# Ten groups of float32 turns on TensorE: products with the identity in 32-column tiles in place of whole transposes

## The chip, the cores and the metric

The kernel runs on one core of one Trainium2 chip. The metric is the device time of one execution in microseconds (us), smaller is better. The profile is one execution recorded by the hardware profiler; its span runs from the first to the last instruction, and the execution's own time is a little longer than the span.

## What is computed

Four sequences of 512 tokens with 128 features go through one post-norm layer: attention with 16 heads of 8 features, a relative-position term that is added to the softmax's result, two layer norms, and then a mixture of 32 small experts of which each token takes its best 4.

```python
attn = softmax(einsum('bhqd,bhkd->bhqk', x @ Wq, x @ Wk) * e ** -0.5)
out = einsum('bhqk,bhkd->bhqd', attn + bias, x @ Wv)     # bias from rel_table
x1 = layernorm(x + layernorm(out, eps=1e-3) * gamma + beta)
sim = (x1 @ hasher_w.T) @ keys.T                          # 32 values a token
w = softmax(top_k(sim, 4))
proj = silu(x1 @ values_down[k]);  o += (proj @ values_up[k]) * w[k]
y = layernorm(x1 + x1 + o * scale)
```

## The kernel before

Four batches are worked through in rounds t = 0 to 3, each of 16 steps u (4 groups of 4 heads, times 4 blocks of 128 keys), and a tail follows. In one step TensorE makes

- four groups of scores `st_ps` (function `scores`, one head each, keys on the partitions). ScalarE takes the exponential of each into `probs` (L801), out of three PSUM banks in turn;
- four groups of scores `sm_ps` (`maximum_scores`) for heads some steps ahead, with the queries on the partitions. VectorE reduces each to its row maximum, `neg_max` (L947), and the two banks of `sm_ps` are used in turn, so each such group waits until the maximum before the last one is taken. The maxima reach the queries' stack later as extra rows, through GpSimd, a small turn ("shift") and a DMA;
- two halves of the product with the values, `ov_ps` (`values`, `value_half`, L1311).

All these products are written by `tiled` (L1253, the matmul itself on L1256): the 128 columns of the weights are cut into four matmuls of 32 columns, each with its own 32 partitions of the result. `whole` (L1266) makes one matmul of 128 columns; `turn` (L1317) is a whole transpose, and `tiled_turn` (L1260) four transposes of 32 columns, which is used for bfloat16 only.

Between these groups stand the "jobs" of round t: `up0` to `up7` are the second layer of the experts for batch t-2, `down0` to `down7` the first layer for batch t-1, `w0` to `w7` spread the experts' weights over rows, `wt` and `shift0` to `shift3` are bfloat16 turns. Three kinds of job are float32 turns of a 128 x 512 tile in four blocks of 128 columns:

- `o0` (eight heads of batch t, one in each of rounds 0 to 3, into `si_ps`) and `o1` (the other eight heads of batch t-1, in rounds 1 to 3, into `mi_ps`). ScalarE copies `ov_ps` to `o_sb` (L812), TensorE turns it (L1378), and VectorE divides by the row sums (`attend`, L953: `rsum`, then `attn`);
- `x1t` (rounds 1 to 3, into `mi_ps`): GpSimd ends the second norm with L523, TensorE turns `x1` (L1390), ScalarE copies it to `x1_t` (L819), and TensorE makes `sim` from it (L1397).

The order on every engine is written out by hand: `JOBS`, `SECOND_JOBS` and `LAST_JOBS` (L165 to L178) say after which step a job stands, `PLACES` and its like where VectorE's steps stand. Round 0 is of kind FIRST, round 1 SECOND, round 2 EVERY and round 3 LAST_ONE. Each engine takes its instructions in order and waits on semaphores. The tail after round 3 has one more `o1` turn (L1577) and one `x1t`.

In the rows a name `out<-a,b` of a matmul lists the moving tile first and then the weights: `si_ps<-ident,o_sb` has `o_sb` as weights and the identity as moving tile. `128*32 128x512` says weights of 128 partitions by 32 columns and 512 moving columns. `x_t` stands for `x1_t` too, and `x` for `x1`.

Of the kernel before, what the change touches and what calls it, by code (L numbers as in the profile page):

```python
# [5 lines left out]
def bass_postln_attention_product_key_ffn(nc, x, w_q, w_k, w_v, rel_table, gamma, beta,  # L6
# [6 lines left out]
    B, S, E = x.shape  # L13
    H = rel_table.shape[1]
    D = E // H
    P = 128
# [33 lines left out]
    with ctx:  # L50
        def sb(name, shape, dt=F32):
            return ctx.enter_context(nc.sbuf_tensor(name, shape, dt))
# [8 lines left out]
        ident, ident_bf = sb("ident", [P, P]), sb("ident_bf", [P, P], BF16)  # L61
# [23 lines left out]
        o_sb = sb("o_sb", [P, S])  # L85
# [10 lines left out]
        x1, x1_t = sb("x1", [P, 2, C, E]), sb("x1_t", [P, S])  # L96
# [99 lines left out]
        def is_misc(n):  # L196

            return n[:2] != "up" and n not in SIDE

        def is_kept(n):  # L200

            return is_misc(n) and n[:4] != "down"

        def is_side(n):

            return n in SIDE
# [20 lines left out]
        def jobs_of(kind):  # L227
            return [n for u in range(U) for half in jobs_at(kind, u) for n in half if here(n, *kind)]

        def job(t, name, counted):  # L230

            before = 0 if counted is is_side else 1
            before += sum(counted(n) for kind in KINDS[:t] for n in jobs_of(kind))
            if t == B + 1:
                return before + 1
            names = jobs_of(KINDS[t])
            return before + sum(counted(n) for n in names[:names.index(name) + 1])
# [17 lines left out]
        def hidden_count(f, j):  # L255
            return f * FJ + (TAIL_DOWN.index(j) if f == B - 1 else j) + 1
# [54 lines left out]
        def pool_at(f, name):  # L311
            if name in LATE_POOL:
                if f < B - 2:
                    return f * len(LATE_POOL) + (LATE_POOL.index(name) + 1)
                return (B - 2) * len(LATE_POOL) + (LATE_POOL_TAIL.index(name) + 1)
            return f * len(POOL_STEPS) + ((POOL_TAIL if f == B - 1 else POOL_STEPS).index(name) + 1)
# [31 lines left out]
        def is0(t):  # L348
            return t == 0
# [873 lines left out]
        def _(pe):  # L1223
# [29 lines left out]
            def tiled(dst, weights, moving, **flags):  # L1253

                for n in range(weights.shape[-1] // TILE):
                    i = nc.tensor.matmul(dst[n * TILE:(n + 1) * TILE], weights[:, n * TILE:(n + 1) * TILE], moving,  # L1256
                                         **flags)
                return i

            def tiled_turn(dst, src, idn):  # L1260

                for n in range(src.shape[-1] // TILE):
                    i = nc.tensor.transpose(dst[n * TILE:(n + 1) * TILE], src[:, n * TILE:(n + 1) * TILE], idn)  # L1263
                return i
# [52 lines left out]
            def turn(dst, src, idn):  # L1317
                return nc.tensor.transpose(dst, src, idn)  # L1318

            def up(f, j, in_round):  # L1320


                if j == 0:

                    count = job(in_round, f"up{FJ - 1}", is_side) - 1
                    if count > 0:
                        pe.wait_ge(side_done, count)
                pe.wait_ge(weighed, hidden_count(f, j))
                for c in range(C):
                    i = tiled(si_ps[:, c * P:(c + 1) * P], hid[:, j, c * P:(c + 1) * P], up_sb[:, j, :],  # L1330
                              start=(j == 0 and c == 0), stop=(j == FJ - 1), skip_group_check=True)
                if j == FJ - 1:
                    i.then_inc(side_ready, 1)

            def tail_up_part(j, c):
                return nc.tensor.matmul(tail_y_bank(c, P), hid[:, j, c * P:(c + 1) * P], up_sb[:, j, :],  # L1336
                                        start=(j == TAIL_UP[0] and c % 2 == 0), stop=(j == TAIL_UP[-1]),
                                        skip_group_check=True)
# [14 lines left out]
            def misc(t, name, kind):  # L1353

                f = t - 1
                if name.startswith("up"):
                    up(t - 2, int(name[2:]), t)
                    return
                bank, ready = (si_ps, side_ready) if is_side(name) else (mi_ps, misc_ready)
                if is0(t) and name == "shift1":  # L1360
                    pe.wait_ge(last_copied, 2)

                if is_side(name):
                    count = job(t, name, is_side) - 1
                    if count > 0:
                        pe.wait_ge(side_done, count)
                else:
                    count = job(t, name, is_kept)
                    pe.wait_ge(misc_done, count - 1 if is_kept(name) else count)
                    names = [n for n in jobs_of(kind) if is_misc(n)]  # L1370
                    last = names[names.index(name) - 1] if names[0] != name else name
                    if last != name and last.startswith("down"):
                        pe.wait_ge(hidden_made, hidden_count(f, int(last[4:])))
                if name.startswith("o"):
                    n = int(name[1:])
                    pe.wait_ge(o_copied, (f if n == PAIRS - 1 else t) * PAIRS + n + 1)
                    for c in range(C):
                        i = turn(bank[:, c * P:(c + 1) * P], o_sb[:, c * P:(c + 1) * P], ident[:])  # L1378
                elif name.startswith("shift"):
                    g = int(name[5:])  # L1380
                    pe.wait_ge(shift_split, (t + 1 if g == 0 else t) * G + g + 1)
                    i = tiled_turn(mi_bf[:, 0:P], shift_parts[:].rearrange("p i n -> p (i n)"), ident_bf[:])
                elif name == "x1t":
                    if t < B:
                        pe.wait_ge(pool_step, pool_at(f, "bscale"))
                    for c in range(C):
                        if t == B:
                            pe.wait_ge(tail_normed, c + 1)
                            bank = mi_ps if c < C // 2 else ov_ps
                        i = turn(bank[:, c * P:(c + 1) * P], x1[:, f % 2, c, :], ident[:])  # L1390
                        if t == B and c == C // 2 - 1:
                            i.then_inc(half_turned, 1)
                elif name == "sim":

                    pe.wait_ge(misc_done, job(t, "x1t", is_kept))
                    for c in range(C):
                        i = tiled(bank[:, c * NE:(c + 1) * NE], x1_t[:, c * P:(c + 1) * P], sim_w[:],  # L1397
                                  start=True, stop=True)
                elif name == "wt":
                    pe.wait_ge(w_split, f + 1)  # L1400
                    pe.wait_ge(spread_made, PARTS)
                    for c in range(C):
                        i = tiled_turn(si_bf[0:PARTS * NE, c * P:(c + 1) * P],
                                       w_parts[:, c].rearrange("p i n -> p (i n)"), ident_bf[:])
                elif name in SPREAD:
                    pe.wait_ge(side_done, job(t, "wt", is_side))
                    i = spread_weights(bank[:, :], int(name[1:]))
                else:
                    j = int(name[4:])
                    if j == 0:  # L1410
                        pe.wait_ge(experts_loaded, 32)
                    i = tiled(mi_ps[:], down_sb[:, j * NJ:(j + 1) * NJ, :].rearrange("k n d -> k (n d)"), x1_t[:],
                              start=True, stop=True)
                i.then_inc(ready, 1)

            def spread_weights(bank, j, product=tiled):
                return product(bank, spread[:, j].rearrange("r n p -> r (n p)"), w_t[:], start=True, stop=True)
# [49 lines left out]
            for n in range(NWIN // P):  # L1467
                i = turn(mi_ps[:, n * P:(n + 1) * P], rel_win[:, n, :], ident[:])
# [13 lines left out]
            for kc in range(C):  # L1482
                i = nc.tensor.matmul(st_ps[:, 2, 0:CG * J * B * D], rel_t[:, LAST:LAST + P],
                                     v_all[:, kc, 0:CG * J].rearrange("p h b d -> p (h b d)"),
                                     start=(kc == 0), stop=(kc == C - 1))
# [85 lines left out]
            f = B - 1  # L1571
# [4 lines left out]
            for c in range(C):  # L1576
                i = turn(mi_ps[:, c * P:(c + 1) * P], o_sb[:, c * P:(c + 1) * P], ident[:])  # L1577
# [44 lines left out]
            for chunks in (FIRST_HALF, SECOND_HALF):  # L1622
                for j in TAIL_UP[-CHUNKED:]:
                    for c in chunks:
                        i = tail_up_part(j, c)
# [23 lines left out]
```

## Time and profile before

| | |
|---|---|
| time, median of 3 runs | 300.7 us (298.92 to 301.14) |
| time of the profiled execution | 301.16 us |
| its span | 299.1 us |
| TensorE busy | 278.4 us, 93% |
| VectorE busy | 235.5 us, 79% |
| ScalarE busy | 197.6 us, 66% |
| GpSimd busy | 130.9 us, 44% |

PE is TensorE's matmuls, PEld its weight loads, DVE is VectorE, ACT ScalarE, POOL GpSimd and SP the engine that issues DMAs. A matmul's duration in the trace reaches from its start to its result in PSUM; the next one starts long before, so what a group costs TensorE is read from its start to the start of the next group, not from its duration. The brackets at the end of a row of a timeline say how long the engine was idle before it and what ended that.

### The profile page before, as it was taken

To read this page: it belongs to the slowest core of one execution; us is meant where nothing else is said; L and a number is where in the kernel's file an instruction comes from. 1 tells how busy PE (TensorE), PEld (TensorE's weight loads), DVE (VectorE), ACT (ScalarE), POOL (GpSimd) and SP (SyncE) were. 2 spreads that over 40 slices of the span, in tenths; PEclk is the share of its full clock that TensorE was granted. 3 is DMA by queue.
4 is the path that set the end of the run, shared out by engine and by line. 5 is a ranking of instruction groups with operands and counts; after the bars stand their busy time and mean duration, and the time that the engine had idled before them with its cause. 6 is when DMAs were issued, how large, how long until landed. Compare 5 with 4: busy or idle time off the path is not lost.

```text
span 299.1 us, 10998 instructions
## 1 busy us (share of the span) xinstructions
PE 278.4 (93%) x4660; PEld 146.7 (49%) x4661; DVE 235.5 (79%) x517; ACT 197.6 (66%) x390; POOL 130.9 (44%) x218
## 2 busy tenths in 40 slices
PE   4969999999999989999999999999999999889992
PEld 2644433444434344444557554445565645367482
DVE  4767899989989978987787799987977864148854
ACT  3652487867776668689864876889656689941620
POOL 8476133110115641137556312189365031885852
PEclk9997999999999999999999999999999999999999
DMA  5565095264051202000403030006100000010011
GB/s 158 154 179 150 9 182 118 40 178 118 2 136 31 79 4 83 4 2 25 139 6 81 4 83 5 1 3 177 24 4 2 6 3 3 2 37 2 2 37 35
DMA packets 18574, 17.27 MB, mean 58 GB/s; under 512 B 6830, under 2 KB 16222, under 8 KB 18526
## 3 DMA queue, kind: packets, MB, share of 16 engines
q1 hardware_dynamic: 17856, 16.39, 21.6%
q8 instruction: 37, 0.61, 0.9%
q10 hardware_dynamic: 670, 0.19, 0.3%
q14 instruction: 11, 0.09, 0.1%
HBM read 12.18 MB, written 4.23 MB: 55 GB/s over the span
## 4 chain that ended last, share of the span: by engine, by line
PE 68%; DVE 12%; DMA 6%; ACT 5%; POOL 4%; issue 3%; SPq 1%; POOLq 0%; DVEq 0%
PE sm_ps L1256 16%; PE st_ps L1256 14%; PE ov_ps L1311 14%; PE mi_ps L1256 6%; PE si_ps L1256 5%; DVE neg_max L947 5%; DMA k_stack<-parts_dram 3%; ACT probs L801 2%; DMA wq_sb<-L_attn_Wq 2%; ACT w_rows L703 1%; PE si_ps L1336 1%; PE mi_ps L1318 1%; PE st_ps L1568 1%; PE sm_ps L1336 1%; PE st_ps L1442 1%
## 5 line engine op out<-in xcount | busy, mean ns | idle before, releaser
L947 DVE TENSOR_REDUCE neg_max<-sm_ps 128x1 f32<-128x512 f32 x256 | 166.4, 685 | 29.2 <-PE sm_ps L1256 24.9
L801 ACT ACTIVATE probs<-st_ps 128x512 f32<-128x512 f32 x256 | 138.2, 610 | 34.0 <-PE st_ps L1256 34.0
L1256 PE MATMUL sm_ps<-k_stack,q_stack 96*32 96x512 bf16 x984 | 97.1, 383 | 3.0 <-DVE neg_max L947 2.1
L1256 PE MATMUL st_ps<-q_stack,k_stack 128*32 128x512 bf16 x1024 | 88.6, 380 | 0.2 <-ACT probs L801 0.2
L1311 PE MATMUL ov_ps<-probs,v_cur 128*32 128x256 f32 x1024 | 76.4, 378 | 0.0
L1256 PEld LDWEIGHTS sm_ps<-k_stack,q_stack 96*32 96x32 bf16 x984 | 26.3, 94 | 50.6 <-DVE neg_max L947 33.9
L533 POOL TENSOR_TENSOR hid<-hid,w_rows 128x512 f32<-128x512 f32 x27 | 34.1, 1278 | 30.7 <-ACT w_rows L703 30.7
L1311 PEld LDWEIGHTS ov_ps<-probs,v_cur 128*32 128x32 f32 x1024 | 31.6, 110 | 22.7 <-ACT probs L801 0.4
L1256 PEld LDWEIGHTS st_ps<-q_stack,k_stack 128*32 128x32 bf16 x1024 | 27.7, 96 | 28.3 <-ACT probs L801 9.1
L1010 DVE SCALAR_TENSOR_TENSOR hid<-tanh_sb,mi_ps 128x512 f32<-128x512 f32 x24 | 16.3, 681 | 15.0 <-ACT tanh_sb L838 15.0
L1256 PE MATMUL mi_ps<-x_t,down_sb 128*32 128x512 f32 x192 | 25.1, 592 | 0.0
L1256 PE MATMUL si_ps<-up_sb,hid 128*32 128x128 f32 x768 | 24.1, 273 | 0.0
L1256 PEld LDWEIGHTS si_ps<-up_sb,hid 128*32 128x32 f32 x768 | 21.3, 110 | 2.7 <-issue 0.3
L838 ACT ACTIVATE tanh_sb<-mi_ps 128x512 f32<-128x512 f32 x24 | 14.6, 610 | 9.3 <-PE mi_ps L1256 9.3
L489 POOL CAST shift_parts<-neg_max 128x16 bf16<-128x16 f32 x16 | 3.1, 196 | 32.6 <-DVE neg_max L947 23.9
L703 ACT ACTIVATE w_rows<-si_ps 128x512 f32<-128x512 f32 x24 | 15.1, 628 | 0.8 <-PE si_ps L1256 0.6
L505 POOL COPY v_cur<-v_all 128x128 f32<-128x128 f32 x16 | 4.5, 290 | 22.0 <-PE ov_ps L1311 21.9
L1256 PE MATMUL si_ps<-w_t,spread 96*32 96x512 bf16 x96 | 9.6, 381 | 1.8 <-ACT w_rows L703 1.8
L703 ACT ACTIVATE x_t<-mi_ps 128x512 f32<-128x512 f32 (+1 forms) x4 | 2.2, 544 | 11.9 <-PE mi_ps L1318 11.9
L553 POOL TENSOR_TENSOR parts<-resid,parts 128x512 bf16<-128x512 f32 x6 | 6.8, 1156 | 6.9 <-ACT parts L703 6.9
L703 ACT ACTIVATE shift_rows<-mi_ps 48x128 bf16<-48x128 bf16 x16 | 4.3, 270 | 6.7 <-PE mi_ps L1263 5.9
L514 POOL TENSOR_SCALAR veps<-mv 128x4 f32<-128x4 f32 x6 | 1.4, 229 | 15.9 <-DVE mv L995 15.9
(189 smaller groups left out, 301.2 us busy)
## 6 DMA issues: line engine op xcount, KB each, us to landing
q_stack<-parts_dram SPq DMA_DIRECT2D x16, 288.0 KB
k_stack<-parts_dram SPq DMA_DIRECT2D x48, 96.0 KB
parts_dram<-parts SPq DMA_DIRECT2D x24, 128.0 KB, 2.4
x_sb<-L_attn_x SPq DMA_DIRECT2D x4, 256.0 KB, 4.6
out<-y_out SPq DMA_DIRECT2D x3, 256.0 KB, 2.3
down_sb<-L_ffn_values_down SPq DMA_DIRECT2D x1, 512.0 KB, 5.7
up_sb<-L_ffn_values_up SPq DMA_DIRECT2D x1, 512.0 KB, 7.9
rel_win<-rel_dram SPq DMA_DIRECT2D x1, 256.0 KB, 2.7
```

The source lines that it names most:

```text
L489: nc.gpsimd.tensor_copy(shift_parts[:, 0, :], m).then_inc(shift_chain, 1)
L505: nc.gpsimd.tensor_copy(v_cur[:, :, g * J:(g + 1) * J, first:first + D], v_all[:, :, g * J:(g + 1) * J, t, :]).then_inc(v_ready, 1)
L533: nc.gpsimd.tensor_tensor(hid[:, j], hid[:, j], w_rows[:, j], ALU.mult).then_inc(weighed, 1)
L553: nc.gpsimd.tensor_sub(parts[:, b, a, 2, :], resid[:, b % 2, a], parts[:, b, a, 1, :]) \
L703: return nc.scalar.activation(dst, src, ACT.Copy, scale=scale)
L801: nc.scalar.activation(probs[:, u % 2, j, :], st_ps[:, score_bank(u * J + j), :], ACT.Exp, scale=SCORE_SCALE).then_inc(probs_ready, 1)
L838: nc.scalar.activation(tanh_sb[:, j % 3, :], mi_ps[:], ACT.Tanh, scale=0.5).then_inc(act_step, 1)
L947: nc.vector.tensor_reduce(neg_max[:, g % 2, col:col + 1], sm_ps[:, c % 2, :], AX.X, ALU.max, negate=True).then_inc(max_ready, 1)
L1010: nc.vector.scalar_tensor_tensor(out=hid[:, j], in0=tanh_sb[:, j % 3, :], scalar=1.0, in1=mi_ps[:], op0=ALU.add, op1=ALU.mult).then_inc(hi ...
L1256: i = nc.tensor.matmul(dst[n * TILE:(n + 1) * TILE], weights[:, n * TILE:(n + 1) * TILE], moving, **flags)
L1311: i = nc.tensor.matmul(ov_ps[j * TILE:(j + 1) * TILE, part], v_cur[:, kc, g * J + j, :], probs[:, u % 2, j, part], start=(g % 2 == 0 and k ...
L1336: return nc.tensor.matmul(tail_y_bank(c, P), hid[:, j, c * P:(c + 1) * P], up_sb[:, j, :], start=(j == TAIL_UP[0] and c % 2 == 0), stop=(j ...
```

## The change

The four float32 transposes of each `o` job and of each `x1t` job in rounds 1 to 3 become matmuls with the same data as weights and the same identity as moving tile, cut by `tiled` into 32 weight columns each: 16 matmuls and 16 weight loads where there were 4 of each. `x1t` of the tail (t == B) keeps the whole transposes, and so do the tail's `o1`, the turns of the start and all bfloat16 turns.

```diff
                     pe.wait_ge(o_copied, (f if n == PAIRS - 1 else t) * PAIRS + n + 1)
                     for c in range(C):
-                        i = turn(bank[:, c * P:(c + 1) * P], o_sb[:, c * P:(c + 1) * P], ident[:])
+                        i = tiled(bank[:, c * P:(c + 1) * P], o_sb[:, c * P:(c + 1) * P], ident[:],
+                                  start=True, stop=True)
...
-                        i = turn(bank[:, c * P:(c + 1) * P], x1[:, f % 2, c, :], ident[:])
+                        if t < B:
+                            i = tiled(bank[:, c * P:(c + 1) * P], x1[:, f % 2, c, :], ident[:], start=True, stop=True)
+                        else:
+                            i = turn(bank[:, c * P:(c + 1) * P], x1[:, f % 2, c, :], ident[:])
```

Ten groups are rewritten: `o0` four times, `o1` three times, `x1t` three times. The other engines keep their instructions and their order.

TensorE around `o0` of round 1, before (a turn among the scores, a `down` job behind it):

```order
L1256 MATMUL sm_ps<-k_stack,q_stack 32x512 x4
L1311 MATMUL ov_ps<-probs,v_cur 32x256 x4
L1256 MATMUL sm_ps<-k_stack,q_stack 32x512 x4
L1318 MATMUL si_ps<-ident,o_sb 128x128 x4
L1256 MATMUL st_ps<-q_stack,k_stack 32x512 x4
L1256 MATMUL sm_ps<-k_stack,q_stack 32x512 x4
```

And in the changed kernel:

```order
L1256 MATMUL sm_ps<-k_stack,q_stack 32x512 x4
L1311 MATMUL ov_ps<-probs,v_cur 32x256 x4
L1256 MATMUL sm_ps<-k_stack,q_stack 32x512 x4
L1256 MATMUL si_ps<-ident,o_sb 32x128 x16
L1256 MATMUL st_ps<-q_stack,k_stack 32x512 x4
L1256 MATMUL sm_ps<-k_stack,q_stack 32x512 x4
```

Nothing changes its place: four matmuls of line 1318 have become sixteen of line 1256 at the same point, and no group around them has moved.

TensorE around `x1t` of round 1, before (the turn of the normed rows, then `sim`, which needs ScalarE's copy of it, and a shift):

```order
L1256 MATMUL sm_ps<-k_stack,q_stack 32x512 x4
L1318 MATMUL mi_ps<-ident,x 128x128 x4
L1256 MATMUL st_ps<-q_stack,k_stack 32x512 x4
L1256 MATMUL sm_ps<-k_stack,q_stack 32x512 x4
L1256 MATMUL mi_ps<-sim_w,x_t 32x32 x16
L1263 MATMUL mi_ps<-ident_bf,shift_parts 32x128 x4
```

And in the changed kernel:

```order
L1256 MATMUL sm_ps<-k_stack,q_stack 32x512 x4
L1256 MATMUL mi_ps<-ident,x 32x128 x16
L1256 MATMUL st_ps<-q_stack,k_stack 32x512 x4
L1256 MATMUL sm_ps<-k_stack,q_stack 32x512 x4
L1256 MATMUL mi_ps<-sim_w,x_t 32x32 x16
L1263 MATMUL mi_ps<-ident_bf,shift_parts 32x128 x4
```

Here too only the turn itself is another; two groups of scores still stand between it and `sim`.

## Rows read from the trace of the kernel before

**Rows 1.** The page: span, and busy time of three engines.

```profile
span 299.1 us, 10998 instructions
PE 278.4 (93%) x4660; PEld 146.7 (49%) x4661; DVE 235.5 (79%) x517; ACT 197.6 (66%) x390; POOL 130.9 (44%) x218
```

**Rows 2.** The page: the chain that ended last, share of the span by engine.

```profile
PE 68%; DVE 12%; DMA 6%; ACT 5%; POOL 4%; issue 3%; SPq 1%; POOLq 0%; DVEq 0%
```

**Rows 3.** Groups by line and shape, TensorE: shapes xcount | busy us, mean ns | idle.

```profile
L1256 PE MATMUL si_ps<-up_sb,hid 128*32 128x128 f32 x768 | 24.1, 273 | 0.0
L1318 PE MATMUL si_ps<-ident,o_sb 128*128 128x128 f32 x16 | 2.6, 286 | 0.0
...
L1256 PEld LDWEIGHTS si_ps<-up_sb,hid 128*32 128x32 f32 x768 | 21.3, 110 | 2.7 <-issue 0.3
```

**Rows 4.** Timeline of TensorE, round 1 around `o0`: start us, us, instruction.

```profile
122.41 0.39 PE L1256 MATMUL sm_ps<-k_stack,q_stack 96*32 96x512 bf16 x4
122.72 0.66 PE L1318 MATMUL si_ps<-ident,o_sb 128*128 128x128 f32 x4
123.31 0.40 PE L1256 MATMUL st_ps<-q_stack,k_stack 128*32 128x512 bf16 x4
...
124.62 0.39 PE L1256 MATMUL st_ps<-q_stack,k_stack 128*32 128x512 bf16 x4
124.95 0.40 PE L1256 MATMUL sm_ps<-k_stack,q_stack 96*32 96x512 bf16 x4
```

**Rows 5.** Timeline of TensorE, round 2, `up` jobs between scores and behind a shift.

```profile
150.43 0.40 PE L1256 MATMUL sm_ps<-k_stack,q_stack 96*32 96x512 bf16 x4
150.66 1.05 PE L1256 MATMUL si_ps<-up_sb,hid 128*32 128x128 f32 x32
151.53 0.39 PE L1256 MATMUL st_ps<-q_stack,k_stack 128*32 128x512 bf16 x4
...
153.71 0.23 PE L1263 MATMUL mi_ps<-ident_bf,shift_parts 128*32 128x128 bf16 x4
153.76 1.04 PE L1256 MATMUL si_ps<-up_sb,hid 128*32 128x128 f32 x32
```

**Rows 6.** Timeline of TensorE, round 2, `o0` behind a shift.

```profile
180.47 0.23 PE L1263 MATMUL mi_ps<-ident_bf,shift_parts 128*32 128x128 bf16 x4
180.64 0.65 PE L1318 MATMUL si_ps<-ident,o_sb 128*128 128x128 f32 x4
```

**Rows 7.** Timeline of TensorE, round 1 behind `o1`.

```profile
87.60 0.63 PE L1318 MATMUL mi_ps<-ident,o_sb 128*128 128x128 f32 x4
88.16 0.62 PE L1256 MATMUL st_ps<-q_stack,k_stack 128*32 128x512 bf16 x8
89.23 0.40 PE L1256 MATMUL sm_ps<-k_stack,q_stack 96*32 96x512 bf16 x4 [0.45 <-DMA k_stack<-parts_dram]
```

**Rows 8.** Timelines of TensorE and ScalarE around `x1t` of rounds 1 and 3.

```profile
107.11 0.63 PE L1318 MATMUL mi_ps<-ident,x 128*128 128x128 f32 x4 [0.49 <-POOL x L523]
107.78 0.60 ACT L703 ACTIVATE x_t<-mi_ps 128x512 f32<-128x512 f32 x1 [1.49 <-PE mi_ps L1318]
108.52 0.46 PE L1256 MATMUL mi_ps<-sim_w,x_t 128*32 128x32 f32 x32 [0.23 <-ACT x_t L703]
...
228.34 0.63 PE L1318 MATMUL mi_ps<-ident,x 128*128 128x128 f32 x4 [0.43 <-POOL x L523]
```

**Rows 9.** Timeline of VectorE at `o0` of round 1, `o1` of rounds 2 and 3.

```profile
122.61 0.68 DVE L947 TENSOR_REDUCE neg_max<-sm_ps 128x1 f32<-128x512 f32 x1
123.42 0.36 DVE L962 RECIPROCAL rsum<-si_ps 128x32 f32<-128x32 f32 x1
...
148.08 0.35 DVE L962 RECIPROCAL rsum<-mi_ps 128x32 f32<-128x32 f32 x1
...
148.86 2.76 DVE L947 TENSOR_REDUCE neg_max<-sm_ps 128x1 f32<-128x512 f32 x4
...
210.49 0.69 DVE L947 TENSOR_REDUCE neg_max<-sm_ps 128x1 f32<-128x512 f32 x1 [0.66 <-PE sm_ps L1256]
```

## The prediction

> **What bounds the kernel now.** I read the page first: TensorE is busy 93% of a span of 299.1 us [rows 1]. Then the chain of waits: 68% of it is TensorE, 12% VectorE, 6% DMA, 5% ScalarE [rows 2]. So time taken from TensorE inside the rounds is worth something, though not everywhere. The groups by shape give the ten turns as a small item: 16 turn matmuls into `si_ps` are 2.6 us of busy time [rows 3], four groups' worth, so some 6.5 us for all ten. What a group costs is read from the timeline, start to start, and that is where the rest of the working comes from.
>
> **The price of one turn now.** In round 1 the score group ahead of `o0` starts at 122.41, the turn at 122.72 and the next score group at 123.31 [rows 4]. A score group ahead of another tiled group takes 0.23 (150.43 to 150.66, [rows 5]), in most places 0.22. Here it takes 0.31: 0.09 is lost on going into the whole-array turn. The turn itself takes 0.59. Behind a shift it is alike: shift to `up` is 0.05 (153.71 to 153.76, [rows 5]), shift to turn 0.17 (180.47 to 180.64, [rows 6]), so 0.12 lost. Going in costs about 0.10. Where TensorE was idle before the turn, or held for a copy, nothing is lost on entry and the turn takes 0.56 (87.60 to 88.16, [rows 7]).
>
> **The price of one turn afterwards.** The trace has this very shape: the `up` jobs are float32 products, 128x32 weights, 128 moving columns, cut by the same function. 32 of them take 0.87 (150.66 to 151.53, [rows 5]), so 16 take 0.435, or 27 ns each, and they start behind a score group or a shift without the loss. One turn thus gives 0.59 + 0.10 - 0.435 = 0.25 us of TensorE where it is busy before, 0.56 - 0.435 = 0.125 where it is not. Its result is hardly sooner than that: last start at 15 x 27 ns = 0.41 plus 0.27 for one matmul [rows 3] is 0.68, against 0.63 to 0.66 from first start to end now [rows 4, 8]. I take them as equal, so a waiting reader gains only the earlier entry, 0.10.
>
> A rule speaks against this step. The Trainium skill, "Perfetto Trace Analysis", section on transposes, says that a logical transpose should be a transpose and not a standard matmul, since the transpose skips the arithmetic; "TensorE: Matmul & The Clock Gate", Terms, calls the transpose mode four times faster for float32. The rows of `up` disagree for tiled weights, where a block of 128x128 in four column tiles is a product in 4 x 27 = 109 ns, against 140 for a whole transpose (0.56 / 4, [rows 7]). By the rule the product would stream four times as long as the transpose and the change would lose; the third rival has the price.
>
> **What each of the ten gives to the end.** What follows the turn decides, and I went through the ten places in the timelines.
>
> 1. `o0`, round 0 (66.4 us): the pattern of [rows 6]. VectorE is short of maxima behind the turn, waits for the next score group, and is the bound afterwards. It starts 0.25 sooner. Kept: 0.25.
> 2. `o1`, round 1: two groups later TensorE waits for `k_stack`, until 89.23 [rows 7]. That transfer was asked for before the turn. Kept: 0.
> 3. `x1t`, round 1: TensorE waits for GpSimd's last norm step, then the path goes turn, ScalarE's copy, `sim`, for which TensorE is idle 0.23 [rows 8]. The faster turn only lengthens this idle time. Between -0.05 and 0.05; taken: 0.
> 4. `o0`, round 1: TensorE gains 0.25, but VectorE is already at the turn's door: its reciprocal starts at 123.42, as the turn ends [rows 9], behind a maximum that lasts until 122.61 + 0.68 = 123.29, and the score group at 124.95 already comes 0.33 behind the one ahead of it, so it waits for VectorE [rows 4]. VectorE can move by 0.13 at most. Kept: 0.13.
> 5. `o1`, round 2: VectorE comes from a maximum to the reciprocal at 148.08 without having waited for the turn, and its four maxima from 148.86 run on until 151.6 [rows 9]; the score groups in this stretch wait for them. An earlier turn moves none of it. Kept: 0.
> 6. `x1t`, round 2 (166.7 us): entered and left like [rows 4], GpSimd done before it, `sim` not waited for. Kept: 0.25.
> 7. `o0`, round 2 [rows 6]: VectorE lags but TensorE has no wait behind it. Kept: 0.25.
> 8. `o1`, round 3 (209.0 us): VectorE was idle 0.66 for the score group behind the turn, at 210.49 [rows 9], and it leads the chain from there. Kept: 0.25.
> 9. `x1t`, round 3: GpSimd decides the entry [rows 8], but three score groups and more stand between it and `sim`, which isn't waited for. Kept: 0.12.
> 10. `o0`, round 3 (243.1 us): no maxima any more; ScalarE is idle behind the turn for the score group and the `down` job and then bounds the rest of the round. Kept: 0.25.
>
> The sum is 0.25 + 0.13 + 0.25 + 0.25 + 0.25 + 0.12 + 0.25 = 1.50 us (places 1, 4, 6, 7, 8, 9, 10). Ten turns at full value would be 8 x 0.25 + 2 x 0.125 = 2.25 us. The profiled execution took 301.16 us (2.1 outside its span), which becomes 299.6; the median of the runs shown is 0.46 lower, 300.7, and becomes 299.2 us. The 240 added instructions (120 matmuls, 120 loads) I cost at nothing: the 32 small matmuls of `sim` all start and end within 0.46 us of waiting [rows 8], so nothing in handing them out is slower than the 27 ns.
>
> The gain on entry is weighed against a rule too. [Rows 4] show 0.09 into the turn and no loss out of it (0.59 against 0.56). The Trainium skill, "TensorEngine Tiling (Array Packing)", Key Properties, says that a change of tiling mode drains the engine. By full drains each busy entry would cost the score group's rest, 0.39 - 0.22 = 0.17, and so would each exit; with 0.17 at eight entries the ceiling would be 2.8 in place of 2.25, and the exit would need a next group at 123.38 and not at 123.31.
>
> **The rivals.**
>
> *Everything is kept (or more).* The waits that I hold against places 2 to 5 could move with TensorE, since the DMA's request, VectorE's steps and the next round all follow from earlier groups: then 2.2 us, 298.5. For it: the chain is two thirds TensorE [rows 2]. Against: rows 7 to 9 show other engines last at these places.
>
> *Little is kept.* Beyond the places above, every later wait for a maximum, for ScalarE's copies of the spread weights or for the stack can take back what an earlier turn gave. For it: VectorE is at 79% over all [rows 1] and gates score groups in every round. Then 0.5 us or less, 300.3.
>
> *The product streams like four transposes.* A score group of 512 columns takes 0.22, so 128 columns stream in 0.055, and `up` with 0.109 for a block goes over them twice. If this product went over them four times, a block would take 0.22 and a turn 0.88: 0.88 - 0.59 - 0.10 = 0.19 more at the eight and 0.32 at the two, 2.2 us in all, 302.9. It is slower, by less than 1%. Against it: `up` needs 0.435 with float32 on both sides. For it only that the identity is a moving tile here, which no tiled row shows.
>
> *The weight loads don't overlap, and it gets slower by over 1%.* The mechanism is in PEld: one load of 128x32 lasts 110 ns [rows 3]. If the loads of one turn stand behind each other, because each block comes back to the same four column tiles, a turn takes 16 x 110 = 1.76 us, 1.1 more than now, and ten cost 11 us, 312. It decides once the spacing of the sixteen is above (0.59 + 0.10) / 16 = 43 ns. Against it: `up` has the same return to the same tiles, at 27 ns, and 768 loads are busy 21.3 us [rows 3], 28 ns each.
>
> **How the numbers follow.** The forecast of 1 to 2 us has a chance of 0.50, everything kept 0.20, little kept 0.22, the slow stream 0.05, loads in a row 0.03. A change of under 1%, about 3 us, is about what a measurement of this kernel can't tell from none, and even the ceiling of 2.25 us is below that; only by a stray median of 0.5 us or more, or by a knock-on that I don't see, would it come out faster by over 1%: 0.11. Slower by over 1% is the last rival and a part of the one before: 0.05. Within 1%: 0.84. The likeliest case alone is 298.7 to 299.7. The range reaches from 297.7, the ceiling with 0.8 for the spread of medians (single runs spread over 2.2 us), to 301.3, which holds little kept and that spread.
>
> **What would show it.** In the changed profile a turn should be 16 matmuls of line 1256 with 0.43 to 0.44 to the next start, and the score group ahead of it 0.22, at eight places. The wait for `k_stack` in round 1 should grow from 0.45 to about 0.6, the idle time before `sim` in round 1 by about 0.12, and VectorE's stretch from 148.08 keep its distance to round 2's start. The span should be near 297.6. The forecast is wrong if a turn's spacing is over 43 ns a matmul, if ScalarE's copy of `x1_t` starts later than 0.67 behind the turn's start, or if the turns are as cheap as said and the span stays within 0.5 us of 299.1, or falls by more than 2.3.

## The result and the profile after

The changed kernel is slower: 304.0 us median of 15 runs against 301.3 for the kernel before, ratio 1.0092 (95% interval 1.0063 to 1.0121), some 2.8 us. Measured again beside its parts it was 303.1 against 300.7, 2.4 us between the medians and 1.8 by the ratio of 1.0061 (1.0024 to 1.0097). 299.2 had been forecast, a gain of 1.5.

The page of the changed kernel: span, and busy time of three engines, against [rows 1].

```profile
span 300.0 us, 11559 instructions
PE 279.6 (93%) x4941; PEld 152.6 (51%) x4941; DVE 235.2 (78%) x517; ACT 197.5 (66%) x390; POOL 131.0 (44%) x218
```

The prediction had 240 more instructions. There are 561, and 281 of them are matmuls: the 16 and 4 of the section on the change are counts of the program, not of the engine. The groups by shape of the changed kernel say where they are (busy us, mean ns | idle):

```profile
L1256 PE MATMUL si_ps<-ident,o_sb 128*32 128x128 f32 x128 | 4.2, 273 | 0.0
...
L1256 PE MATMUL mi_ps<-ident,x 128*32 128x128 f32 x96 | 3.2, 274 | 0.9 <-POOL x L523 0.9
L1256 PE MATMUL mi_ps<-ident,o_sb 128*32 128x128 f32 x96 | 3.2, 273 | 0.1
```

128 for four turns is 32 for a turn: 4 blocks x 4 column tiles x 2. A float32 product that stands once in the program is two matmuls on the engine, while a float32 transpose is one ([rows 3]: 16 for four turns of four blocks). 10 x (32 - 4) = 280 is what was added. [Rows 3] had said it of `up` too: 768 for the 24 `up` jobs are 32 for a job, and the 32 of [rows 5] are one job, not two. `sim` had shown it too, with x16 in the program's order and x32 in [rows 8].

The timeline of TensorE in the changed kernel, at `o0` of round 1, of [rows 4], and at `o0` of round 2, of [rows 6]:

```profile
121.61 0.39 PE L1256 MATMUL sm_ps<-k_stack,q_stack 96*32 96x512 bf16 x4
121.83 1.05 PE L1256 MATMUL si_ps<-ident,o_sb 128*32 128x128 f32 x32
122.70 0.39 PE L1256 MATMUL st_ps<-q_stack,k_stack 128*32 128x512 bf16 x4
...
124.00 0.39 PE L1256 MATMUL st_ps<-q_stack,k_stack 128*32 128x512 bf16 x4
124.48 0.40 PE L1256 MATMUL sm_ps<-k_stack,q_stack 96*32 96x512 bf16 x4
...
180.34 0.23 PE L1263 MATMUL mi_ps<-ident_bf,shift_parts 128*32 128x128 bf16 x4
180.40 1.04 PE L1256 MATMUL si_ps<-ident,o_sb 128*32 128x128 f32 x32
181.27 0.39 PE L1256 MATMUL st_ps<-q_stack,k_stack 128*32 128x512 bf16 x4
```

The turn takes 0.87 to the next start where 0.435 was forecast, and 0.59 was before. The entry came as forecast: 0.22 behind a score group in place of 0.31, 0.06 behind a shift in place of 0.17 (only at place 10, where it is 0.12, less was gained). The spacing is 27 ns, as forecast, but of 32 matmuls. Read from the start of the group ahead to the start of the group behind, TensorE pays 0.17 to 0.19 more at six turns (0.87 - 0.69 = 0.18), 0.30 to 0.32 at three (0.87 - 0.56 = 0.31; places 2, 3 and 9, where it was idle or held ahead of the turn) and 0.23 at place 10, 2.27 us in all.

The result of a turn comes later as well. It ends 1.05 to 1.08 behind the turn's first start, against 0.63 to 0.66 [rows 4, 8]. VectorE at `o0` of round 1 [rows 9], then ScalarE and TensorE at `x1t` of round 1 [rows 8], in the changed kernel:

```profile
121.81 0.69 DVE L947 TENSOR_REDUCE neg_max<-sm_ps 128x1 f32<-128x512 f32 x1
122.95 0.36 DVE L962 RECIPROCAL rsum<-si_ps 128x32 f32<-128x32 f32 x1 [0.45 <-PE si_ps L1256]
...
106.98 0.60 ACT L703 ACTIVATE x_t<-mi_ps 128x512 f32<-128x512 f32 x1 [1.96 <-PE mi_ps L1256]
...
105.84 1.08 PE L1256 MATMUL mi_ps<-ident,x 128*32 128x128 f32 x32 [0.49 <-POOL x L523]
...
107.72 0.46 PE L1256 MATMUL mi_ps<-sim_w,x_t 128*32 128x32 f32 x32 [0.36 <-ACT x_t L703]
```

VectorE, which came to the turn as it ended, now stands idle 0.45 before it, and the score group that waited 0.33 behind its predecessor comes 0.48 behind it (124.00 to 124.48). ScalarE's copy of `x1_t` starts 1.14 behind the turn's start, against 0.67, and TensorE's idle time before `sim` has grown from 0.23 to 0.36.

### How the stretches are compared

The profiled spans differ by only 0.9 us, less than the runs say. The missing part lies ahead of the first turn, in instructions that are the same in both. The stretches of granted clock of the kernel before and then of the changed one (columns: stretch; busy us of PE, PEld, DVE, ACT, POOL; PEclk; DMA share, GB/s):

```profile
22.00:30.00 8.00, 8.00 (x102) 4.08 (x101) 6.37 (x11) 2.10 (x3) 5.51 (x5) 0.79 0.60 151
```

```profile
22.00:30.00 8.00, 8.00 (x124) 4.24 (x128) 7.89 (x14) 2.23 (x4) 6.13 (x8) 1.00 0.67 162
```

The execution of before had TensorE at its lower level (1.2 GHz) for part of these 8 us, the changed one didn't, and it came to the shift ahead of the first turn at 65.08 in place of 66.19. The other traces go the same way: those with 1.00 in these 8 us reach that shift at 65.00 and 65.34, those with 0.68 to 0.81 between 65.95 and 68.35. From there to the tail's `o1` turn (265.39 and 266.20) both run at the full clock. That stretch is 199.20 us before, 201.12 in the changed kernel and 201.11 in a second profile of it: it repeats to 0.01, and it is 1.92 longer. I use it below, cut at the start of the group ahead of each turn. The places are numbered as in the prediction; each figure is the length of its piece less that of the kernel before, in us. The third and fourth columns of figures are experiments told below.

| place | forecast | changed kernel | half turns | read columns |
|---|---|---|---|---|
| 1 `o0` r0 | -0.25 | +0.17 | -0.26 | -0.20 |
| 2 `o1` r1 | 0 | -0.34 | +0.29 | +0.82 |
| 3 `x1t` r1 | 0 | +0.48 | +0.03 | -0.01 (whole) |
| 4 `o0` r1 | -0.13 | +0.33 | -0.08 | +0.01 |
| 5 `o1` r2 | 0 | +0.16 | -0.25 | -0.20 |
| 6 `x1t` r2 | -0.25 | +0.18 | -0.25 | +0.01 (whole) |
| 7 `o0` r2 | -0.25 | +0.19 | -0.25 | -0.17 |
| 8 `o1` r3 | -0.25 | +0.18 | -0.26 | -0.17 |
| 9 `x1t` r3 | -0.12 | +0.33 | -0.12 | -0.01 (whole) |
| 10 `o0` r3 | -0.25 | +0.24 | -0.14 | -0.11 |
| sum | -1.50 | +1.92 | -1.29 | -0.03 |

### The profile page after: what moved, and what is told of

It reads as the page before. It is cut to its first block, busy times and chain, and to the rows that moved or that the text cites. A ratio compares the mean times of both kernels' runs of the same rounds, so it can differ in the third digit from the quotient of the medians.

```text
span 300.0 us, 11559 instructions
## 1 busy us (share of the span) xinstructions
PE 279.6 (93%) x4941; PEld 152.6 (51%) x4941; DVE 235.2 (78%) x517; ACT 197.5 (66%) x390; POOL 131.0 (44%) x218
## 4 chain that ended last, share of the span: by engine, by line
PE 70%; DVE 12%; ACT 5%; DMA 4%; POOL 4%; issue 3%; SPq 1%; POOLq 0%; DVEq 0%
PE sm_ps L1256 16%; PE st_ps L1256 14%; PE ov_ps L1311 14%; PE mi_ps L1256 8%; PE si_ps L1256 7%; DVE neg_max L947 6%; ACT probs L801 2%; DMA wq_sb<-L_attn_Wq 1%; DMA k_stack<-parts_dram 1%; ACT w_rows L703 1%; PE si_ps L1336 1%; PE st_ps L1241 1%; PE st_ps L1572 1%; PE sm_ps L1336 1%; PE st_ps L1446 1%
## 5 line engine op out<-in xcount | busy, mean ns | idle before, releaser
L1311 PEld LDWEIGHTS ov_ps<-probs,v_cur 128*32 128x32 f32 x1024 | 32.3, 110 | 22.1 <-ACT probs L801 0.4
L1256 PEld LDWEIGHTS st_ps<-q_stack,k_stack 128*32 128x32 bf16 x1024 | 28.7, 96 | 26.2 <-ACT probs L801 8.2
L636 POOL TENSOR_TENSOR sdiff<-sim,top 128x128 f32<-128x128 f32 x3 | 1.2, 407 | 15.9 <-DVE top L1016 15.9
```

Of the source, the lines that this page charges most:

```text
L1311: i = nc.tensor.matmul(ov_ps[j * TILE:(j + 1) * TILE, part], v_cur[:, kc, g * J + j, :], probs[:, u % 2, j, part], start=(g % 2 == 0 and k ...
```

## The experiments

### The change once more, and its two parts

The changed kernel again, then only the outputs as tiled products (`x1t` whole), then only the normed rows (`o` whole). The second kernel's edit to the changed one:

```diff
-                        if t < B:
-                            i = tiled(bank[:, c * P:(c + 1) * P], x1[:, f % 2, c, :], ident[:], start=True, stop=True)
-                        else:
-                            i = turn(bank[:, c * P:(c + 1) * P], x1[:, f % 2, c, :], ident[:])
+                        i = turn(bank[:, c * P:(c + 1) * P], x1[:, f % 2, c, :], ident[:])
```

The third takes back the other half:

```diff
-                        i = tiled(bank[:, c * P:(c + 1) * P], o_sb[:, c * P:(c + 1) * P], ident[:],
-                                  start=True, stop=True)
+                        i = turn(bank[:, c * P:(c + 1) * P], o_sb[:, c * P:(c + 1) * P], ident[:])
```

> The changed kernel once more, beside its parts on one chip. Theory A (each float32 matmul of the source is two matmuls on the engine, so a turn is 32 matmuls and 0.87 us against 0.69 or 0.56): about 2.1 us above before, ratio 1.007, a turn of 0.87 in the trace. Theory B (the turns cost little at the end and most of the loss is half-clock stretches): the ratio varies with the granted clock, and the spans at equal clock are within 0.7 us of before.

> Only the seven output turns are tiled products, the three turns of normed rows are whole transposes. Theory A: 7 x 0.18 = 1.3 us above before, less about 0.2 at the one turn with a wait for a transfer behind it: 1.1 to 1.3, ratio 1.004. Theory B: within 0.5 us of before at equal clock.

> Only the three turns of normed rows are tiled products. Theory A: 0.87 - 0.56 = 0.31 at the two where TensorE was idle before, 0.18 at the third: 0.8 us above before, ratio 1.0027. Theory B: nothing measurable, since GpSimd decides the entry at two of the three.

Measured against before: the change 1.0061 (1.0024 to 1.0097), outputs only 1.0076 (1.0046 to 1.0106), rows only 1.0027 (0.9993 to 1.0060). In the stretch the outputs alone add 1.24 us and the rows alone 0.95, both without place 2; together they make 2.19, and the changed kernel has 2.26 without that place. So the parts add up. For the rows alone the interval holds 1, so that their loss is shown by the stretch and not by the runs. Theory B falls: half-clock stretches at the start move single spans by a us or two, but 1.92 and 1.91 stand in two traces at full clock.

Place 2 has to be read by itself. It holds the wait for `k_stack`, which differs from execution to execution: 0.45 in [rows 7], 0.86 and 1.33 in two of the experiments below, and none in the six other traces. The kernel with rows only is the same program as before up to this place, with a whole transpose here, and had no wait. TensorE at place 2, rows only and then the changed kernel:

```profile
90.31 0.62 PE L1256 MATMUL st_ps<-q_stack,k_stack 128*32 128x512 bf16 x8
90.76 0.39 PE L1256 MATMUL sm_ps<-k_stack,q_stack 96*32 96x512 bf16 x4
```

```profile
87.52 0.64 PE L1256 MATMUL st_ps<-q_stack,k_stack 128*32 128x512 bf16 x8
87.95 0.43 PE L1256 MATMUL sm_ps<-k_stack,q_stack 96*32 96x512 bf16 x4
```

Start to start that is 0.45 and 0.43, against 1.07 in [rows 7]. So the -0.34 in the table is a wait that happened to be absent and hides a loss. Without the wait the piece is 0.67 shorter than before with whole transposes (rows only), and 0.33 or 0.34 shorter with the tiled turn (both profiles of the change, and outputs only): there the turn costs 0.33, as the 0.31 has it. With that the change costs 2.26 + 0.33 = 2.59 us where the transfer isn't late, and the outputs alone 1.24 + 0.34 = 1.58, inside the interval of their ratio (1.4 to 3.2 us), where 1.24 lies below it.

### The product without the tiles

```diff
-                        i = tiled(bank[:, c * P:(c + 1) * P], o_sb[:, c * P:(c + 1) * P], ident[:],
+                        i = whole(bank[:, c * P:(c + 1) * P], o_sb[:, c * P:(c + 1) * P], ident[:],
                                   start=True, stop=True)
```

and the same for `x1t` in the rounds.

> All ten turns are products with the identity, but whole, 128 weight columns each, so the tiles are taken away and the product is left. Theory A (the product's two passes cost, not the tiles): 8 matmuls at 0.112 us as in the tail's whole products, 0.90 for a turn, and the loss of 0.10 on entry stays: 0.31 above before at eight, 0.34 at two, 3.2 us in all, ratio 1.010. Rival (the cutting into 32 columns costs): 0.56 to 0.6 for a turn and a time like before.

Measured 305.1 against 300.7, ratio 1.0153 (1.0107 to 1.0199). The timeline of TensorE in this kernel, `o0` of round 1:

```profile
124.79 0.39 PE L1256 MATMUL sm_ps<-k_stack,q_stack 96*32 96x512 bf16 x4
125.11 1.16 PE L1267 MATMUL si_ps<-ident,o_sb 128*128 128x128 f32 x8
126.20 0.40 PE L1256 MATMUL st_ps<-q_stack,k_stack 128*32 128x512 bf16 x4
```

Eight matmuls for four blocks: the doubling comes with the product, not with the tiles. They are 0.136 apart, though, not 0.112, so a turn takes 1.09 and not 0.90. The stretch is 4.39 longer than before where theory A had 3.2, and the runs say 4.6 (3.2 to 6.0). The groups by shape give the load of such a block, 191 ns, where a whole transpose has 140 and a tile 110:

```profile
L1267 PEld LDWEIGHTS si_ps<-ident,o_sb 128*128 128x128 f32 x32 | 3.9, 191 | 0.7 <-issue 0.6
```

The tail's whole products have loads as long (192) and a closer spacing (four in 0.45); why, I didn't test. The score group ahead takes 0.32 again, as ahead of a whole transpose. Of the three ways to turn a tile, then, each with its entry: whole transposes 0.69, tiled products 0.87, whole products 1.19. The cutting is the good part of the change and the product the bad one.

### The turn that the prediction had priced

Each of the ten turns makes only blocks 0 and 1 of four, so that it is 16 matmuls; the other half of the turned tile is left out.

```diff
-                    for c in range(C):
+                    for c in range(C // 2):
                         i = tiled(bank[:, c * P:(c + 1) * P], o_sb[:, c * P:(c + 1) * P], ident[:],
```

and the same for `x1t` in the rounds.

> Each of the ten tiled turns makes only two of its four blocks of 128 columns, so half of the turned tile is left out. 16 matmuls, 0.435: this is the turn as the prediction had counted it. If the accounting by places held and only the count was wrong, the stretch from the first turn to the tail's is 1.5 us shorter than before, ratio 0.995. Rival (costs are kept everywhere, gains are lost to the engine that comes next): less than 0.8 us shorter, ratio 0.9975 or more. Other rival: nearly all of 2.25 is kept, ratio 0.9925.

Measured 299.8 against 301.3, ratio 0.9942 (0.9905 to 0.9980). The stretch is 1.29 shorter, and 1.58 without place 2 (here with a wait of 0.86), where 1.50 had been forecast. The timeline of TensorE in this kernel, `o1` of round 2 (place 5), and VectorE at the same place:

```profile
147.70 0.39 PE L1256 MATMUL sm_ps<-k_stack,q_stack 96*32 96x512 bf16 x4
147.92 0.61 PE L1256 MATMUL mi_ps<-ident,o_sb 128*32 128x128 f32 x16
148.36 0.60 PE L1256 MATMUL st_ps<-q_stack,k_stack 128*32 128x512 bf16 x8
...
150.87 0.40 PE L1256 MATMUL sm_ps<-k_stack,q_stack 96*32 96x512 bf16 x4
```

```profile
148.15 0.69 DVE L947 TENSOR_REDUCE neg_max<-sm_ps 128x1 f32<-128x512 f32 x1 [0.62 <-PE sm_ps L1256]
148.75 0.35 DVE L962 RECIPROCAL rsum<-mi_ps 128x32 f32<-128x32 f32 x1
149.13 0.49 DVE L966 TENSOR_TENSOR attn<-mi_ps,rsum 128x128 f32<-128x128 f32 x2
149.54 2.51 DVE L947 TENSOR_REDUCE neg_max<-sm_ps 128x1 f32<-128x512 f32 x4
```

The turn is 0.44, as the sum had it. VectorE does stay in step with the maximum ahead of the turn, and yet the 0.25 isn't lost here: the piece up to the next turn is 0.25 shorter. The score group that VectorE holds up (150.87) had slack behind it, and the four maxima take 2.51 in place of 2.76: before, the second of them started 0.83 behind the first, behind the score group that it reads, and here 0.60.

### Twice the turn

```diff
-                    for c in range(C):
+                    for c in 2 * tuple(range(C)):
                         i = tiled(bank[:, c * P:(c + 1) * P], o_sb[:, c * P:(c + 1) * P], ident[:],
```

and the same for `x1t` in the rounds.

> Each of the ten tiled turns is made twice over, into the same bank; nothing is left out. One more turn is 32 matmuls, 0.87 us. If TensorE's time is the path at all ten places, the stretch from the first turn to the tail's grows by 8.7 us over the changed kernel, ratio to before 1.037. If other engines hide part of it, as at the wait for the stack in round 1, less: 7 us or under.

Measured 312.4 against 301.3, ratio 1.0372 (1.0336 to 1.0408). Over the changed kernel the stretch grows by 9.69 us. Nine of the ten pieces grow by 0.84 to 0.89, as long as one more turn of 0.87; none is hidden, not even at place 2, which had no wait in either trace. The tenth, place 8, grows by 1.87, because TensorE once stands idle without a releaser:

```profile
219.09 0.38 PE L1311 MATMUL ov_ps<-probs,v_cur 128*32 128x256 f32 x1 [0.89 <-issue]
```

No other trace of this case has that hole, and its cause stays open.

### Only the columns that are read

`attend` reads 9 of every 16 columns of a turned block: 8 features of a head and its row sum. The turn needs no others. On top of the kernel with the outputs only:

```diff
+            def read_columns(a):
+                return a.rearrange("p (n w) -> p n w", w=HALF_TILE)[:, :, 0:D + 1]
...
-                        i = tiled(bank[:, c * P:(c + 1) * P], o_sb[:, c * P:(c + 1) * P], ident[:],
-                                  start=True, stop=True)
+                        i = tiled(read_columns(bank[:, c * P:(c + 1) * P]), o_sb[:, c * P:(c + 1) * P],
+                                  read_columns(ident[:]), start=True, stop=True)
```

> A turn that could beat both: the output turns stay tiled products, but make only the 9 of every 16 columns that are read afterwards (8 features and the row sum of a head), 72 moving columns in place of 128; the turns of normed rows are whole transposes as before. Theory A1 (the 27 ns from matmul to matmul are two passes over the moving columns): 15 ns each, 0.49 for a turn of 32, so 0.59 + 0.10 - 0.49 = 0.20 less than before at six places, 1.2 us in all, ratio 0.996. Theory A2 (the 27 ns are the weight load, 110 ns shared by four tiles): the turn stays at 0.87 and the time is that of the kernel with tiled outputs only, 1.0076 of before.

Measured 300.1 against 301.3, ratio 0.9954 (0.9922 to 0.9985). The groups by shape and the timeline of TensorE in this kernel, the latter at `o0` of round 1 and behind `o1` of that round:

```profile
L1256 PE MATMUL si_ps<-ident,o_sb 128*32 128x72 f32 x128 | 2.8, 226 | 0.0
...
L1256 PEld LDWEIGHTS si_ps<-ident,o_sb 128*32 128x32 f32 x128 | 2.3, 109 | 0.2
```

```profile
122.39 0.69 PE L1256 MATMUL si_ps<-ident,o_sb 128*32 128x72 f32 x32
122.90 0.40 PE L1256 MATMUL st_ps<-q_stack,k_stack 128*32 128x512 bf16 x4
...
89.01 0.40 PE L1256 MATMUL sm_ps<-k_stack,q_stack 96*32 96x512 bf16 x4 [1.33 <-DMA k_stack<-parts_dram]
```

Still 32 matmuls and 32 loads of 109 ns, but 0.51 for the turn: 16 ns apart where it was 27. So the spacing follows the moving columns (theory A1), and the loads hide at this pace too. Without place 2 the stretch is 0.85 shorter than before, where 1.2 had been expected; place 4 keeps nothing, as VectorE starts on the turn's result only 0.04 sooner than before (0.97 behind the start of the score group ahead in place of 1.01). In this profile the wait for `k_stack` happened to be 1.33, so that the whole stretch is only 0.03 shorter, while the runs give 1.4 us.

## Why the prediction was wrong

- **The price afterwards: the step that failed.** "32 of them take 0.87, so 16 take 0.435" is true, but 16 was the count in the program, where the trace counts two matmuls for each. I compared the program's count of the turn with the trace's count of `up`. One `up` job has the same 16 products in the program as one turn, so its 0.87 was the price of a turn. With it the sum's own terms give 0.87 - 0.69 = +0.18 at eight and 0.87 - 0.56 = +0.31 at two. That is 2.06 us; the stretch measured 1.92, which was in part luck with the wait at place 2: 2.26 without that place, and 2.59 with it where no trace has the wait. Of the 2.59 TensorE pays 2.27 at the turns; 0.16 at place 3 and 0.14 at place 4 come on top. The count of eight and two was off as well: place 2 was held for a copy before the turn, so it belonged to those with 0.56.
- **The third rival, given 0.05, was the right one.** It had the product go over the columns four times, 0.055 us each, with 0.88 for a turn and 2.2 us for the ten. Measured are 0.87 and 1.9 to 2.6. What I held against it, `up` with 0.109 for a block, is 0.217 once the 32 are one job: four times 0.055, which fits two matmuls that go over them twice each. With 72 columns it is 0.51 / 4 = 0.13 for a block, and four times 0.22 x 72 / 512 is 0.12. A whole transpose takes 0.14 for a block, as long as its load of 140 ns; that the load is what holds it wasn't tested. The Trainium skill had the direction right in both places that the prediction set aside. "TensorE: Matmul & The Clock Gate", Terms, calls the transpose mode four times faster for float32; in time the runs show less, 0.14 against 0.217 for a block in tiles and 0.27 as a whole product. "Perfetto Trace Analysis", Transposes, advises a transpose and not a standard matmul. For a whole turn the trace agrees with 0.69 against 0.87; with only the read columns the product was the cheaper one, 0.51.
- **The entry** was right where TensorE was busy: 0.22 in place of 0.31 and 0.06 in place of 0.17. At place 10 it went from 0.17 to 0.12 only.
- **"A waiting reader gains the earlier entry"** was wrong by the same count. At place 4 the result comes 1.05 behind the first start, 0.39 later than before, less 0.09 of entry: 0.30, and the piece grew by 0.33 where TensorE alone would give 0.19. At place 3, with nothing to gain on entry, it comes 0.45 later (1.08 against 0.63), and the piece grew by 0.48 and not 0.32. Where a reader waits for the turn, its latency is the price and not its throughput.
- **The places** held in the main when tried with the turn they were made for: -1.58 against -1.50 without place 2. That the sums agree so closely is partly luck, since the misses offset each other: place 5 kept all 0.25 where I had said none, place 10 kept 0.14 of 0.25, and place 4 0.08 of 0.13. Going through the places had mattered for a gain; for the loss nearly every place paid in full.
- **Place 2** was called lost to a transfer, from one trace. The wait is absent in six of the nine traces, and there the change cost 0.33 at this place.
- **The added instructions at nothing** held for handing them out: the spacing stayed at 27 ns with 32 and with 64 in a row.
- **Loads in a row**, the last rival, fell: 32 loads of 109 ns lie within a turn of 0.51.

## What to carry to other kernels

Before a price is taken from a shape in the trace, divide its count in the trace by how often the program issues it: for float32 products here that gives two, for float32 transposes one. Take the price for a whole job of the same content (one `up` job for one turn) and the count can't go wrong. Where a transpose's output is read in part, a product with only the read columns of the identity can be cheaper than the transpose of the whole block (0.51 against 0.69 here). A transpose of the read columns alone wasn't tried. And before a place is written off for a wait, look whether a second trace of the same kernel has that wait: here most had none.

## What the runs showed of the hardware

- A float32 product in 32-column tiles is two matmuls for each that the program has, 27 ns apart for 128 moving columns and 16 ns for 72, while the loads last 110 ns each.
- A whole float32 transpose of a block is one matmul, 0.14 apart with a load of 140 ns; as a whole product the block is two, 0.136 apart with a load of 191.
- Going from 32-column tiles to a whole matmul cost some 0.10 in all kernels that did it (a score group 0.31 to 0.33 in place of 0.22, a shift 0.17 in place of 0.06), and going back 0.03 at most (0.59 against 0.56).
- The rounds repeat to 0.01 us in 200 in two profiles of one kernel at full clock, as long as one transfer isn't late (its wait was 0 in six traces, and 0.45, 0.86 and 1.33 in three). Ahead of the rounds the traces differ with how long TensorE is at its lower level: with a granted clock of 0.79 between 22 and 30 us the shift ahead of the first turn came 1.1 us later than with 1.00. That this makes a good part of the spread of 2 to 6 us among the runs of one kernel is likely, since the longer ones mostly have the lower mean clock, but wasn't tested.
